# A new order for the matmuls of a causal-attention block: searched on other engine intervals, with the last value projection moved behind the row selection of chunk 2

## The reference

```python
qkv = einsum('bsd,ed->bse', x, W_qkv)      # 16 heads of 8 features each
q = _rope(q, positions); k = _rope(k, positions)
scores = einsum('bhqd,bhkd->bhqk', q, k) / sqrt(8)
scores = where(causal, scores, -inf)
out = einsum('bhqk,bhkd->bhqd', softmax(scores), v)
x = _layernorm(x + out.reshape(B, S, 128) @ W_o.T)
w = simulate_quantize_int4(kernel)         # one scale for the matrix
x = _layernorm(x + x @ w + bias + (x @ a) @ b)
```

## Time and profile before

| | |
|---|---|
| median of 3 runs | 437.37 us |
| the profiled execution | 437.25 us, its span 435.5 us |
| busy in the span | PE 412.0, DVE 374.5, ACT 313.5, POOL 114.6 us |
| mean granted TensorE clock | 0.985 |

### The profile page before, as it was taken

One profiled execution on the slowest core, in us unless ns is written; L12 is line 12 of the kernel. 1 busy time (PEld: TensorE's weight loads), 2 busy tenths in 40 slices (PEclk: granted clock), 3 DMA queues, 4 the chain that ended last, 5 costly groups with the idle time before them and its releaser, 6 DMA issues.

```text
span 435.5 us, 8512 instructions
## 1 busy us (share of the span) xinstructions
PE 412.0 (95%) x3250; PEld 202.5 (47%) x3250; DVE 374.5 (86%) x487; ACT 313.5 (72%) x552; POOL 114.6 (26%) x184
## 2 busy tenths in 40 slices
PE   5999799999999999999999999999999999999992
PEld 2556444354335453465453544444354354436651
DVE  2878889999999989998899999999989977657586
ACT  2454765785776877686877797978786888898761
POOL 8879610202212111212011213003003001205534
PEclk9999889999999999999999999999999999999997
DMA  7522322200000000022200022200000000000011
GB/s 236 187 99 78 133 65 69 74 25 3 0 2 3 2 2 4 2 70 60 75 3 2 6 81 62 59 2 2 2 2 2 2 2 2 3 2 3 3 50 49
DMA packets 12200, 16.57 MB, mean 38 GB/s; under 512 B 2444, under 2 KB 7324, under 8 KB 12160
## 3 DMA queue, kind: packets, MB, share of 16 engines
q1 hardware_dynamic: 11072, 15.75, 11.6%
q0 software_dynamic: 1088, 0.28, 0.4%
HBM read 10.37 MB, written 5.24 MB: 36 GB/s over the span
## 4 chain that ended last, share of the span: by engine, by line
PE 78%; DVE 15%; ACT 4%; issue 2%; DMA 1%; SPq 0%; DVEq 0%; ACTq 0%
PE ps L1296 28%; PE ps L1280 19%; PE ps L1227 17%; DVE pmax L1038 13%; PE ps L1195 3%; ACT probs L961 3%; PE ps L1305 2%; PE ps L1241 2%; PE ps L1237 1%; PE ps L1211 1%; PE ps L1324 1%; PE ps L1201 1%; DMA x_sb<-in_L_attn_x_dram 1%; PE ps L1251 1%; PE ps L1328 1%
## 5 line engine op out<-in xcount | busy, mean ns | idle before, releaser
L1038 DVE TENSOR_REDUCE pmax<-ps 128x2 f32<-128x1024 f32 (+3 forms) x273 | 318.4, 1214 | 35.3 <-PE ps L1227 20.0
L961 ACT ACTIVATE probs<-ps 128x512 f32<-128x512 f32 (+4 forms) x485 | 282.1, 655 | 81.9 <-PE ps L1280 80.8
L1280 PE MATMUL ps<-qS,kS 64*128 64x512 f32 (+3 forms) x664 | 149.9, 404 | 2.8 <-DVE pmax L1038 2.3
L1296 PE MATMUL ps<-probs,vP 128*9 128x512 f32 (+3 forms) x1328 | 146.4, 520 | 0.2
L1227 PE MATMUL ps<-kS,qS 64*128 64x512 f32 (+3 forms) x640 | 137.1, 418 | 6.6 <-DVE pmax L1038 2.3
L1280 PEld LDWEIGHTS ps<-qS,kS 64*128 64x128 f32 x664 | 78.4, 187 | 81.0 <-ACT probs L961 45.6
L1227 PEld LDWEIGHTS ps<-kS,qS 64*128 64x128 f32 x640 | 64.9, 186 | 68.5 <-DVE pmax L1038 29.1
L868 POOL TENSOR_SCALAR_AFFINE_SELECT probs<-probs 128x512 f32<-128x512 f32 x64 | 40.4, 635 | 123.3 <-ACT probs L961 123.2
L877 POOL DMA_DIRECT2D qS<-mrows x34 | 19.6, 578 | 163.5 <-DVE mrows L1058 163.5
L1296 PEld LDWEIGHTS ps<-probs,vP 128*9 128x9 f32 x1328 | 21.1, 88 | 39.2 <-issue 26.8
L1241 PEld LDWEIGHTS ps<-causal_x,ident_x 64*128 64x128 f32 x188 | 17.9, 186 | 0.0
(11 more groups left out here) (120 smaller groups left out, 188.5 us busy)
## 6 DMA issues: line engine op xcount, KB each, us to landing
qS<-q_parts SPq DMA_DIRECT2D x52, 64.0 KB
kS<-k_parts SPq DMA_DIRECT2D x52, 64.0 KB
cs<-rope_tables_dram SPq DMA_DIRECT2D x4, 512.0 KB, 6.7
q_parts<-qp SPq DMA_DIRECT2D x4, 512.0 KB, 2.8
k_parts<-kp SPq DMA_DIRECT2D x4, 512.0 KB, 2.8
x_sb<-in_L_attn_x_dram SPq DMA_DIRECT2D x4, 256.0 KB, 5.8
out_dram<-rot SPq DMA_DIRECT2D x2, 256.0 KB, 2.4
qS<-mrows POOLq DMA_DIRECT2D x30, 8.0 KB, 1.8
```

The costliest lines, as they stand in the source:

```text
L961: nc.scalar.activation(probs[:, J % PRING, heads[0]:heads[-1] + 1:3 - len(banks), lo:hi], src, ACT.Exp, scale=float(DK) ** -0.5).then_inc( ...
L1038: nc.vector.tensor_reduce(dst, src, AX.X, ALU.max).then_inc(unit_free, 1)
L1280: last = nc.tensor.matmul(ps[:, bank, at:at + w], kS[rows, b, j // TPC, hp, (j % TPC) * TOK:(j % TPC + 1) * TOK], qS[rows, b, c, hp, lo:hi ...
L1296: last = nc.tensor.matmul(bank_of(("PV", n, 0))[VW * h:VW * h + VC, lo:hi], vP[:, j, HG * g + h, :], probs[:, J % PRING, h, lo:hi], start= ...
```

## The change

Four things change.

1. `TURNS` is another string, so all engines have another order from the first maxima on. `D` stands in it 84 times and not 91, so there are 492 exponentials and not 485 for the same elements.
2. In `PROLOGUE` the value projection of chunk 3 stands behind the row selection of chunk 2 and not ahead of it.
3. `Course` has other intervals, and counts the copies that ACT makes for `E`, `V`, `X`, `P` and `H`. They act only through the bank choice and the places of the loads.
4. There is code that would let ACT copy some scores out and POOL take their maxima. It is steered by `OUT_OF`, an empty table, so no instruction comes from it.

```diff
+OUT_OF = {}
+COPIED_OUT = [(n, unit) for n in OUT_OF for unit in units(n)[OUT_OF[n][0]:-len(OWN[TASKS[n][2:]]):OUT_OF[n][1]]]
...
-            (35.0, 1.9, "P", 3, 1), (35.0, 0, "R", 3, 1), (35.0, 1.1, "V", 1), (36.0, 0, "D", 2), (37.0, 1.1, "V", 2), (40.0, 1.1, "V", 3),
-            (44.0, 0.9, "E", 2, 0), (45.0, 0.9, "E", 2, 1), (45.0, 0, "H", 3, 0), (45.0, 0, "T", 3, 0), (48.0, 0, "H", 3, 1),
+            (35.0, 1.9, "P", 3, 1), (35.0, 0, "R", 3, 1), (35.0, 1.1, "V", 1), (36.0, 0, "D", 2), (37.0, 1.1, "V", 2),
+            (44.0, 0.9, "E", 2, 0), (45.0, 0.9, "E", 2, 1), (47.0, 1.1, "V", 3), (45.0, 0, "H", 3, 0), (45.0, 0, "T", 3, 0), (48.0, 0, "H", 3, 1),
...
-    LOAD, COLUMN, GAP, ENTRY, EXIT = 0.096, 1 / 2400, 0.007, 0.122, 0.082
-    TO_ACT, TO_DVE, TO_PE, ACT_TO_PE = 0.302, 0.181, 0.149, 0.18
-    DVE_FIX, ACT_FIX, M_WORK, O_WORK, PLACED, VFIX = 0.064, 0.05, 0.51, 0.49, 1.25, 0.079
+    LOAD, COLUMN, GAP, ENTRY, EXIT = 0.1, 1 / 2400, 0.016, 0.115, 0.08
+    TO_ACT, TO_DVE, TO_PE, ACT_TO_PE = 0.29, 0.17, 0.13, 0.13
+    DVE_FIX, ACT_FIX, M_WORK, O_WORK, PLACED, VFIX = 0.155, 0.09, 0.6, 0.6, 1.25, 0.094
+    COPIES = {"E": 1.2, "V": 0.5, "X": 0.5}
...
+            if kind in self.COPIES and e[0] > 0:
+                self.act = max(self.act, self.pe) + self.COPIES[kind]
...
 TURNS = (
-    "ppppppppppppppAppppppApppAAppApAApMpppAAppApAppApppAAppApAApAppMppppApASASDASSSASSASVSAASDVASVSAVSASDASSASAASSSVADASAASA"
+    "pppppppppppppApppppppAppAApppAApApAApppppApApAAppppMAApppApAApppppppADASASSMSASASVSASASVSSASSASSASSVASVSASSASVASSASSASSS"
...
```

More of the change, by code:

```diff
@@ L314, in take @@
                     end = self.product(hl, w, ready)
-            self.reduced(end, maxima_time(n, unit))
+            if (n, unit) in COPIED_OUT:
+                self.act = max(self.act, end + self.TO_ACT, self.outs[0]) + 0.09 + 2 * CH / 1200
+                self.give(self.act + self.ACT_TO_PE, self.took)
+                self.pool = max(self.pool, self.act + 0.25) + POOL_MAXIMA
+                self.outs, self.pooled = (self.outs[1], self.pool + 0.1), self.pool + 0.2
+            else:
+                self.reduced(end, maxima_time(n, unit))
             if unit == units(n)[-1]:
-                self.dve += 0.22
+                self.dve = max(self.dve, self.pooled) + 0.22
                 self.due += ((self.dve + self.TO_PE, "M", n),)
@@ L472 @@
     last.update((b, e) for b in HELD.get(e, ()))
+OUT = {e[1:]: i for i, e in enumerate(e for e in SCHEDULE if e[0] == "A" and e[1:] in COPIED_OUT)}
 STEP = {e[1:3]: i for i, e in enumerate(e for e in SCHEDULE if e[0] == "S" and e[3] == 0)}
@@ L558, in attention_block @@
         rows = [[rot[:, w, i, :] for w in range(2) for i in range(3)], [cs[:, c, w, :] for c in range(NC) for w in range(2)]]
+        outs = [xT[:, 2 * i:2 * i + 2, :] for i in range(2)]
         onT, resT = [r[0] for r in rows], [r[1] for r in rows]
@@ L589, in attention_block @@
         wq_step = sem("wq_step")
+        copied_out = sem("copied_out")
+        pool_maxima = sem("pool_maxima")
         centre_set = sem("centre_set")
@@ L869, in mask_probs, with slots_of, maxima @@
                                    pattern=[[0, HG], [1, TOK]], channel_multiplier=-1).then_inc(masked, 1)
+            def slots_of(n, unit):
+                _, _, first, end = TASKS[n]
+                return pmax[:, :, unit[3], AREA[n] + PLACE[first, end][unit[2]] * SLOTS + 3 + unit[1]]
+            def maxima(n, unit):
+                at = OUT[n, unit]
+                pool.wait_ge(slots_set, 1)
+                if PRIOR[n] is not None:
+                    pool.wait_ge(nmax_done, PRIOR[n] + 1)
+                pool.wait_ge(copied_out, at + 1)
+                nc.gpsimd.tensor_reduce(slots_of(n, unit), outs[at % 2], AX.X, ALU.max).then_inc(pool_maxima, 1)
             def load_maxima(n):
@@ L886, in _ @@
             for e in SCHEDULE:
+                if e[0] == "A" and e[1:] in COPIED_OUT:
+                    maxima(*e[1:])
                 if e[0] == "M":
@@ L962, in exponentials, with copy_scores @@
                                      scale=float(DK) ** -0.5).then_inc(exp_done, 1)
+            def copy_scores(n, unit):
+                e, at = ("A", n, unit), OUT[n, unit]
+                act.wait_ge(unit_done, UNIT[e])
+                if at == 0:
+                    prep_freed(act, ("V", NC - 1))
+                if at >= 2:
+                    act.wait_ge(pool_maxima, at - 1)
+                nc.scalar.copy(outs[at % 2], unit_banks(e)).then_inc(copied_out, 1)
             def flush_o(n):
@@ L976, in _ @@
             for e in SCHEDULE:
+                if e[0] == "A" and e[1:] in COPIED_OUT:
+                    copy_scores(*e[1:])
                 if copied_by_act(e):
@@ L1148, in _ @@
                     nc.vector.tensor_reduce(wst[:, 0:1], ffn_sb[:, :], AX.X, ALU.max, apply_absolute_value=True).then_inc(wq_step, 1)
-                if e[0] == "A":
+                if e[0] == "A" and e[1:] not in COPIED_OUT:
                     row_max(*e[1:])
```

28 lines of the change are left out of this document (19 added, 9 removed).

## The result

The changed kernel takes 439.44 us in the median of four runs (438.56 to 439.78), and the kernel before 437.39 on the same chip (four runs, 437.16 to 437.58): the ratio is 1.0044 [1.0027, 1.0061]. It is 2.05 us slower; 438.6 was forecast. The profiled execution took 439.78 us with a span of 438.0, 2.5 more than before.

What follows compares the result with a forecast made beforehand. PE bounds the opening and DVE, 94% busy, the stretch from 60 to 345 us. Opening +2.1 and middle -0.9, with clock and closing at 0, gave +1.2 on 437.25: 438.6 us, 8-in-10 range 435.7 to 440.6.

Steps and rivals of the forecast that it cites:

- term e: Start of task 2: DVE's two small steps for task 1's maxima rows now stand between maxima, costing 0.65 us.
- Term a: Opening: first maxima, now ahead of chunk 1's key projection, wait for DVE's kS copy; 1.1 us late (0.5 to 1.3).
- Term b: Opening: chunk 3 turned and projected back to back, so PE idles for ACT's xT copy; 0.75 us (0.4 to 0.9).
- Term c: Opening: two maxima units ahead of chunk 3's key projection, the second waiting for a bank pair; 0.7 us (0 to 1.1).
- Term d: End of opening: the last value projection moves into PE's hole behind the key selection, giving 1.1 us back.
- The clock: Behind the opening: the granted clock falls to half again, for the same 1.9 us as before, so 0 change.
- The middle: Maxima of the middle: two peaks flatten, a third of 5.8 us won, 1.0 lost in a fuller stretch; -0.9 us.
- The closing: From the last values to the last norm: same events on DVE, so 0, with 0.5 us either way.
- Costs nothing: Whole kernel: empty table and new planner intervals add no instruction, seven more exponentials fit ACT's free time; 0 us.
- clock kept: Behind the opening: PE's clock stays up and DVE's 1.86 us wait goes; 436.7 us, chance 20%.
- The middle pays more: Middle: the flatter mix removes most of two peaks, 3.5 us, with the clock falling as before; 436.1 us, chance 20%.
- the middle pays nothing: Middle gains 0 and task 1's rows arrive late, costing 1 us; 440.5 us, chance 18% with a worse middle.

Runs made afterwards that it cites:

- the whole opening: Kernel before with its first 68 events in the changed kernel's order, banks of before kept; 440.36 us, ratio 1.0059.
- the two tail edits: Changed kernel with the old order from task 16's second maxima on (439.75 us), or with only task 13's norm moved behind `O` of task 16 (438.97 us).
- the reversed opening: Changed kernel, its own banks kept, with the opening order of the kernel before; 441.81 us, ratio 1.0096.
- the full mend: Changed kernel with the first maxima and two task 1 maxima units moved back, and task 13's norm moved behind `O` of task 16; 438.28 us, ratio 1.0017.
- the mend of a and b: Changed kernel with the first maxima back behind chunk 1's key projection and two maxima units back between chunk 3's turning and projection; 439.06 us.

## Why the prediction came out as it did

The total came out near, 439.44 for 438.6, and the sum behind it did not. Forecast and profile by place, in us against before:

| stretch | forecast | profile |
|---|---|---|
| to the 20th maxima (terms a to d) | +1.45 | +1.70 |
| 20th to 26th (term e 0.65, clock 0) | +0.65 | -1.54 |
| 26th to 248th | -0.9 | +1.07 |
| behind the 248th | 0 | +1.31 |
| sum | +1.2 | +2.54 |

The 2.2 us that the clock made too dear hid two thirds of the 3.3 us by which the middle and the end came out too cheap. That is luck, and two of the prediction's own three signs of being wrong came: the clock stayed up, and the middle was longer.

- **The opening: near in sum, by errors that cancel.** The prediction's 2.1 holds term e, which stands behind the 20th maxima; ahead of them it is 1.45, and 1.79 was measured from the copy on. Term a was right: a wait of 0.94, and 1.09 alone for 1.1. Term b was too small: a wait of 0.68 for 0.75, but 1.34 alone. The turning then no longer overlaps with the work that was ahead of the projection; that this is the rest of it is my reading, not shown. Term c: a wait of 0.63 for 0.7, but only 0.25 is left for it when a, b and d are taken from the 2.57 of the whole opening. Term d failed: it fills the hole as said, and was worth 0.11 for 1.1 where it could be tried alone. My step "in a stretch without holes" was wrong: there was none because the projection itself covered a wait for DVE's banks. And with its own banks the order costs 1.8 where it costs 2.6 with those of before: 0.8 back, which no term had. Term e was not tried apart.
- **The clock: failed in the profiled run.** I took it that the clock falls again, 0. It stayed at 2.4 GHz through the opening, and from the 20th to the 26th maxima the kernel won 1.54 us back, near the 1.9 of the rival. With the same order and a half clock of 3.4 us the win was 0.38 and 0.44 (the two tail edits), so 3.4 us of it cost 1.1. For the 6.8 us of before, the two kernels with the value projection moved give 1.83 (an estimate, since their banks differ from the 22nd maxima on). So the clock can account for all of the 1.54. Whether the new order keeps the clock up, or this run did, is open: the same order fell in two other profiles.
- **The middle: failed.** Forecast -0.9, measured +1.07 from the 26th to the 248th maxima, and 1.05, 1.01, 1.12 and 1.00 in four other kernels with this order (the reversed opening, the two tail edits, the full mend). Both peaks did lose, 1.71 and 1.89 us, more than the third of 5.8 that I took. The fuller stretch lost 1.49 for 1.0. What sank it lay elsewhere: the 26th to the 44th lose 1.77 and the 80th to the 92nd 1.22. The first I had not counted. The second I had counted, 17 products and 6 value steps for 17.5 and 4, and had put at nothing. All five kernels also have nearly the same new banks, 788 of 838 of them other than before. The new order with the old intervals was never run, so how much of the 1.07 is order and how much banks is open.
- **The closing: failed in size.** Forecast 0 with 0.5 either way, since the last events are the same on DVE. The last 44 instructions of DVE are; the norm of task 13 stands directly ahead of them, which the forecast left out. From the 248th maxima to the end it is +1.31. In the two kernels with the same tail in which the clock held for 8.2 and 10.2 us of the closing (the reversed opening, the mend of a and b) it is +0.21 and +0.28, so about 1.0 of it is the clock that fell 3.5 us into the closing. The rest is small, and the norm's place in DVE's queue can account for it (0.6 in one pair of profiles, 0.2 in the other).
- **"Costs nothing", the intervals: not shown.** They put no instruction in. What they did to the new order no run tells; with the order of before they cost 10.6 us, and I had set no bound to that.

If all of the 1.54 is put down to the clock, the part of order and banks is 1.70 + 1.07 + 0.25 = 3.0 us; the clock gave 1.5 back behind the opening and took 1.0 at the end.

Of the rivals, *clock kept* described the profiled run's 26th maxima and not its total. *The middle pays more* is out by the middle's +1.07. Of the third, *the middle pays nothing* came, and *rows come late* did not, since among PE's waits in the profile none is for the rows of task 1. Two slips of the working change little: 18.2 lies 2.7 above 15.5 and not 2.5, and the second rival takes 3.4 off where it says 3.5.

The Trainium skill ("TensorE: Matmul & The Clock Gate", Part 1) prices a half clock by its length times one less the ratio. These traces show less, as the prediction had it. The two mended kernels have the same order there, and the one with 17.1 us of half clock lost 4.44 us between the 20th and 32nd maxima where the other won 1.22: 5.7 us. The 3.4 us above cost 1.1, and the 6.8 us 1.8. By the rule these would be 8.5, 1.7 and 3.4. So it is about a third of the length; that DVE has scores in hand for part of it would explain this, and was not tested.

**Open.** What decides where the clock falls: one kernel shows mean clocks of 0.976 and of 0.996. What makes the copy into `kS` start up to 1.05 us apart behind the same instructions. And which of a few hundred banks, or of the moved loads, cost the 3 to 10 us of a wrong plan.

## What to carry to other kernels

In a pipeline whose next stage is full, a hole in the opening reaches the end whole, so look for what a moved instruction was covering at its old place before counting its new place as a gain. When a search rearranges an order, compare progress (the start of the n-th piece of the bounding engine's work) over the whole span, and not the stretches that stood out; and measure it from the last instruction ahead of the edit, or the run's own start is counted as the edit's. Buffers planned from modelled times belong to the order they were planned with: move an event by hand and keep the plan, or search again.

## What the runs showed of the hardware

Other PSUM banks and other places for the loads, with every compute instruction in its place, moved the time by 10.6 us (2.4%). Holes of the opening were handed on over 350 us nearly whole: 1.09 us was 1.14 at the last maxima, and 1.34 was 1.30. The kernel before ran its 435 us at mean clocks of 0.985 (12.8 us at half, by its profile) to 0.995 (about 4.3, worked out), and another was at half for 17.1 us right behind its opening alone; the price there was about a third of the length. One run each of two kernels took 708 and 1183 us at a mean clock of 1.00; neither has a profile, and the cause is open.
